# In the first stage's ScalarE step, the normalisation of quad q is put ahead of the message of quad q-1

## The chip, the cores and the metric

The kernel runs on 1 core of a Trainium2 chip. The metric is the device time of one execution in microseconds. The engines are TensorE (PE in the rows; PEld is its weight load), VectorE (DVE), ScalarE (ACT), GpSimd (POOL) and SyncE (SP). Each has its own instruction queue, works through it in order, and meets the others at semaphores only.

## The reference

Two graph layers on 6250 nodes of 256 features and 106,250 edges (`src`, `dst`, a weight each). The first one is a message network:

```python
x1 = concatenate((h[src], h[dst], weight))
msg = silu(x1 @ mW1 + mb1)
msg = layer_norm(msg, ln_g, ln_b)
msg = silu(msg @ mW2 + mb2)
agg = segment_sum(msg, src)
y = silu(concatenate((h, agg)) @ uW1 + ub1) @ uW2 + ub2
x = layernorm(x + h + y)
```

The second takes the mean of `x[src]` over each `dst`, multiplies by `W.T`, adds `b`, applies relu, adds it to `x` and normalises again.

## The kernel before, in words

The edges are sorted by `dst`. A preparation counts them into blocks of 125 nodes, and makes a table `p_tab` of each node's product with one part of mW1, and keeps the products with the other part in `big`. Edges are taken in tiles of 128, and four tiles are a **quad** (`QT` = 4; `QUADS` quads, 220 of them by the count of L973).

The change is in the first stage, the loop over quads. `message_loop(eng, step)` issues, for each engine, the step of every q from -2 to QUADS+2, in unrolled steps at the ends and in loops of four steps between. All buffers named below have two halves, the parity of the quad. For a quad q:

- POOL gathers four times 128 rows of `p_tab` into `gat` (`gather_0`, L572), one step ahead.
- PE multiplies a one-hot by `big` (`expand`, L762), one step ahead; DVE adds it to the gathered rows and writes `act` (`pre`, L1346), at the end of its step before.
- ACT applies silu to `act` in two halves (`silu`, L949).
- DVE takes the statistics (`bn_stats`, L1356), then a chain of small instructions on 128x4 values (`inverse_root`, L360 to L376) ends in `shift` (L1380). Between the links of the chain stand other jobs of DVE's step: `stage` and `one_hot` for quad q+2, `buckets` for q+1, `place` for q-1 (the rows to which the messages go), and `message_sum`.
- ACT applies scale and shift (`norm`, four instructions, L955).
- PE transposes `act` in eight pieces (`norm_columns`, L749) in its step q+1; ACT brings the two halves to `zt` with gain and bias (its own `norm_columns`, L964); PE multiplies by mW2 (`main`, L774 and L775).
- ACT applies the last silu and writes `msg` (`message`, L972 and L973); POOL scatters it to `msg_tab` (`place_messages`, L582).

PE's step q is, in order: `norm_columns(q-1)`, `expand(q+1)`, `rank(q)` (L736, L738), `main(q-1)`. ACT's step q is: silu half 0 of q, half 0 of `norm_columns(q-1)`, silu half 1, half 1 of `norm_columns(q-1)`, `message(q-1)`, `norm(q)`. `message(q-1)` waits until `main(q-1)` has ended (`mm`), and until the scatters of quad q-3 have landed (`add`). `norm(q)` waits for `shift` of q.

From quad `SWITCH` (108) the sorted messages of the first part are also summed beside the steps, in **visits**, from quad 112 on. Three visits stand in every even step, two in every odd one (`SHARE`). A visit is a load by SP (L469), two one-hots on DVE (L1461), four products on PE (`collect`, L802) and an addition on DVE (`message_sum`, L1481). PE has its collects behind `norm_columns`, behind `expand` and, the third, behind `main`. DVE has its three sums behind the statistics, in the chain, and, the third, right ahead of `shift`.

Behind the loop come the rest of the visits, the update network on 50 blocks, the second layer and the output. The change touches none of these.

Of the kernel before, what the change touches and what calls it, by code (L numbers as in the profile page):

```python
# [28 lines left out]
QUADS = -(-(TILES + BLOCKS - 1) // QT)  # L29
# [31 lines left out]
def gnn(nc, x, src, dst, edge_w, mW1, mb1, ln_g, ln_b, mW2, mb2, uW1, ub1, uW2, ub2, W, b, out):  # L61
# [13 lines left out]
    with ExitStack() as ctx:  # L75
# [269 lines left out]
        def live(q, n):  # L345

            return not isinstance(q, int) or 0 <= q < n
# [5 lines left out]
        def later(q, n):  # L353

            return not isinstance(q, int) or q >= n
# [570 lines left out]
        def _(ac):  # L926
# [20 lines left out]
            def silu(q, par, v):  # L947
                ac.wait_ge(s["pre"], 2 * q + v + 1)
                nc.scalar.activation(act[:, par, 2 * v:2 * v + 2, :], act[:, par, 2 * v:2 * v + 2, :], ACT.Silu)\  # L949
                    .then_inc(s["silu"], 1)  # L950

            def norm(q, par):
                ac.wait_ge(s["shift"], q + 1)
                for u in range(QT):
                    last = nc.scalar.activation(act[:, par, u, :], act[:, par, u, :], ACT.Identity,  # L955
                                                bias=shift[:, par, u:u + 1], scale=nwt[:, par, 3, u:u + 1])
                last.then_inc(s["norm"], 1)

            def norm_columns(q, par, h):

                ac.wait_ge(s["ztr"], 2 * q + h + 1)
                if h == 0 and later(q, 2):
                    ac.wait_ge(s["mm"], q - 1)
                nc.scalar.activation(zt[:, par, h, :], ps[:, PZ + h, :], ACT.Identity,  # L964
                                     bias=gb[:, h, 1:2], scale=gb[:, h, 0:1]).then_inc(s["zev"], 1)

            def message(q, par):
                ac.wait_ge(s["mm"], q + 1)
                if later(q, 2):
                    ac.wait_ge(s[f"add{par}"], half_count(q - 2) * (16 * QT))  # L970
                    ac.sem_inc(s_turn_act, 1)
                nc.scalar.activation(msg[:, par, :, D], vkey[:, bass.ds(q * QT, QT)], ACT.Copy).then_inc(s["msg"], 1)  # L972
                nc.scalar.activation(msg[:, par, :, 0:D],  # L973
                                     ps[:, PM:PM + 2, :].rearrange("p b (u d) -> p (b u) d", u=2), ACT.Silu)\
                    .then_inc(s["msg"], 1)

            def step_0(q, par, group):
                for i in range(2):
                    if live(q, QUADS):
                        silu(q, par, i)  # L980
                    if live(q - 1, QUADS):
                        norm_columns(q - 1, 1 - par, i)
                if live(q - 1, QUADS):
                    message(q - 1, 1 - par)
                if live(q, QUADS):
                    norm(q, par)
            ac.wait_ge(s_weights, 16 * 14)
            message_loop(ac, step_0)

            ac.wait_ge(s["qexp"], QUADS)  # L990
# [635 lines left out]
```

## Time and profile before

| | us |
|---|---|
| median of 3 runs | 5003.13 (5003.01 to 5013.02) |
| the profiled execution's own time | 5005.49 |
| its span | 5003.7 |
| PE busy in the span | 3701.3 (74%) |
| DVE busy | 2915.6 (58%) |
| POOL busy | 2583.9 (52%) |
| ACT busy | 1379.0 (28%) |

The mean granted clock of TensorE over the span was 0.858 of full speed. The messages L973, one in each quad, start between 258.3 and 3177.8 us, so the loop over quads holds some 2920 us of the span. In the page's slices PE is busy in seven tenths nearly throughout it, no other engine in more than six tenths. In the chain that ended last PE has 62% of the span and ACT 10%, of which `norm` (L955) has 8%. A busy share is a mean over steps of some 12 to 14 us; which engine is waited for is seen in the order of time in one such step.

### The profile page before, as it was taken

To read this page: it belongs to the slowest core of one execution; us is meant where nothing else is said; L and a number is where in the kernel's file an instruction comes from. 1 tells how busy PE (TensorE), PEld (TensorE's weight loads), DVE (VectorE), ACT (ScalarE), POOL (GpSimd) and SP (SyncE) were. 2 spreads that over 40 slices of the span, in tenths; PEclk is the share of its full clock that TensorE was granted. 3 is DMA by queue.
4 is the path that set the end of the run, shared out by engine and by line. 5 is a ranking of instruction groups with operands and counts; after the bars stand their busy time and mean duration, and the time that the engine had idled before them with its cause. 6 is when DMAs were issued, how large, how long until landed. Compare 5 with 4: busy or idle time off the path is not lost.

```text
span 5003.7 us, 78162 instructions
## 1 busy us (share of the span) xinstructions
PE 3701.3 (74%) x15597; PEld 2734.1 (55%) x15598; DVE 2915.6 (58%) x11562; ACT 1379.0 (28%) x2573; POOL 2583.9 (52%) x2725
## 2 busy tenths in 40 slices
PE   6877777777777777777777777677894777777775
PEld 3455555555555566666666666455583444444444
DVE  5655555555555666666666666466555555545555
ACT  0244444444444444444444444100030000000003
POOL 0066556565565555555555555100004777777753
PEclk9987777777777889999889999899997888888888
DMA  2333222332332444444444444666403333333323
GB/s 54 103 93 93 90 92 91 92 94 90 91 92 92 124 133 138 137 138 136 137 136 139 137 139 135 160 190 185 143 1 114 105 105 105 105 104 105 105 77 104
DMA packets 281644, 563.52 MB, mean 113 GB/s; under 512 B 57407, under 2 KB 128659, under 8 KB 281583
## 3 DMA queue, kind: packets, MB, share of 16 engines
q0 software_dynamic: 124416, 343.51, 22.6%
q1 hardware_dynamic: 150772, 212.91, 15.0%
q10 hardware_dynamic: 6395, 6.40, 0.6%
q8 instruction: 25, 0.41, 0.0%
q14 instruction: 36, 0.29, 0.0%
HBM read 423.51 MB, written 139.08 MB: 112 GB/s over the span
## 4 chain that ended last, share of the span: by engine, by line
PE 62%; DMA 10%; ACT 10%; issue 9%; DVE 4%; DVEq 2%; POOL 1%; SPq 1%; ACTq 1%; POOLq 0%
PE ps L774 16%; PE ps L762 10%; ACT arena L955 8%; PE ps L881 8%; PE ps L802 8%; PE ps L749 8%; DMA arena<-x_tab,esrc 7%; PE ps L884 2%; PE ps L775 2%; PE ps L711 2%; PE ps L832 2%; DMA arena<-msg_tab 1%; PE ps L738 1%; POOL arena L604 1%; DMA arena<-x_tab 1%
## 5 line engine op out<-in xcount | busy, mean ns | idle before, releaser
L582 POOL DMA_INDIRECT msg_tab<-arena,sidx x880 | 865.3, 983 | 892.8 <-ACT arena L973 662.0
L572 POOL DMA_INDIRECT arena<-p_tab,idx x880 | 864.3, 982 | 556.6 <-DVE idx L1328 288.4
L604 POOL DMA_INDIRECT arena<-x_tab,esrc x832 | 789.2, 949 | 299.1 <-issue 142.9
L749 PE MATMUL ps<-ident,arena 128*128 128x128 f32 x1760 | 388.3, 393 | 727.7 <-ACT arena L955 727.7
L881 PE MATMUL ps<-arena 128*125 x1760 | 661.3, 464 | 337.8 <-DMA arena<-x_tab,esrc 296.1
L774 PE MATMUL ps<-w,arena 128*128 128x256 f32 x3520 | 894.7, 387 | 0.9 <-ACT arena L964 0.9
L1356 DVE BATCH_NORM_STATS2 bst<-arena 128x6 f32<-128x256 f32 x880 | 331.2, 418 | 879.2 <-ACT arena L949 879.1
L749 PEld LDWEIGHTS ps<-ident,arena 128*128 128x128 f32 x1760 | 308.5, 204 | 813.2 <-ACT arena L955 613.7
L802 PE MATMUL ps<-arena 128*125 128x256 f32 x2180 | 640.6, 430 | 122.2 <-DVE arena L1461 92.7
L881 PEld LDWEIGHTS ps<-arena 128*125 128x125 f32 x1760 | 378.9, 225 | 603.3 <-issue 516.9
L774 PEld LDWEIGHTS ps<-w,arena 128*128 128x128 f32 x3520 | 608.4, 193 | 125.0 <-ACT arena L964 1.3
L1575 DVE TENSOR_TENSOR arena<-ps,arena 125x257 f32 x880 | 374.7, 426 | 516.3 <-PE ps L881 471.5
L762 PE MATMUL ps<-arena 126*128 x1760 | 586.9, 493 | 8.9 <-DVE arena L1346 5.8
L802 PEld LDWEIGHTS ps<-arena 128*125 128x125 f32 x2180 | 431.7, 215 | 275.1 <-issue 107.6
L762 PEld LDWEIGHTS ps<-arena 126*128 126x128 f32 x1760 | 441.0, 258 | 94.5 <-issue 9.9
L972 ACT ACTIVATE arena<-vkey 128x4 f32 (+1 forms) x220 | 45.9, 209 | 1562.2 <-PE ps L775 1562.2
L955 ACT ACTIVATE arena<-arena,shift,nwt 128x256 f32<-128x256 f32 x880 | 454.2, 589 | 10.0 <-DVE shift L1380 5.7
L1461 DVE TENSOR_SCALAR arena<-nodes,cboff,arena 128x125 f32<-128x125 bf16 x1090 | 337.2, 357 | 118.3 <-DMA arena<-msg_tab 46.5
L884 PE MATMUL ps<-identh 128*128 128x512 bf16 x880 | 396.0, 450 | 0.0
L964 ACT ACTIVATE arena<-ps,gb 128x512 f32<-128x512 f32 x440 | 340.6, 774 | 135.7 <-PE ps L749 135.6
L1027 ACT ACTIVATE arena<-ps 128x250 f32<-128x250 f32 x50 | 18.6, 373 | 1128.7 <-DVE cnt L1591 1128.7
L1481 DVE TENSOR_TENSOR arena<-ps,arena 125x256 f32 x545 | 229.8, 422 | 157.9 <-PE ps L802 154.4
(199 smaller groups left out, 4248.0 us busy)
## 6 DMA issues: line engine op xcount, KB each, us to landing
arena<-msg_tab SPq DMA_DIRECT2D x545, 264.0 KB
arena<-loc_tab SPq DMA_DIRECT2D x220, 125.0 KB
arena<-p_tab,idx POOLq DMA_INDIRECT x880
msg_tab<-arena,sidx POOLq DMA_INDIRECT x880
arena<-x_tab,esrc POOLq DMA_INDIRECT x832, 2.8
arena<-x_tab SPq DMA_DIRECT2D x50, 128.0 KB, 2.0
arena<-in_x_dram SPq DMA_DIRECT2D x50, 112.0 KB
p_tab<-arena SPq DMA_DIRECT2D x50, 112.0 KB
```

What stands on the lines that cost most here:

```text
L572: pool.indirect_dma_start(out=gat[:, par, u, 0:D], out_offset=None, in_=p_tab[:, :], in_offset=bass.IndirectOffsetOnAxis(ap=idx[:, par, u: ...
L582: pool.indirect_dma_start(out=msg_tab[part][:, :], in_=msg[:, par, u, :], in_offset=None, out_offset=bass.IndirectOffsetOnAxis(ap=sidx[:, ...
L604: pool.indirect_dma_start(out=ring[:, tile % RING, 0:D], out_offset=None, in_=x1_tab[:, :], in_offset=bass.IndirectOffsetOnAxis(ap=esrc[:, ...
L749: last = nc.tensor.transpose(ps[:, PZ + h, u * P:(u + 1) * P], act[:, par, u, h * P:(h + 1) * P], ident[:, :])
L762: last = nc.tensor.matmul(ps[:, PP + u // 2, u % 2 * D:(u % 2 + 1) * D], hott[0:NB + 1, par, u, :], big[0:NB + 1, bass.ds(blocks_[u], 1), ...
L774: nc.tensor.matmul(to, zt[:, par, h, u * P:(u + 1) * P], w2[:, h, :], start=h == 0, stop=False)
L802: last = nc.tensor.matmul(ps[0:NB, bank, 0:D], chot[:, j % 2, i, :], crow[:, j % CSLOTS, i, 0:D], start=i == 0, stop=i == 1)
L881: nc.tensor.matmul(ps[0:NB, u, 0:CW], same1[:, par, u, :], ring[:, bass.ds(at[u], 1), :].rearrange("p a c -> p (a c)"), start=True, stop=T ...
L884: nc.tensor.matmul(ps[:, PK, :], identh[:, :], identh[:, :].unsqueeze(1).to_broadcast([P, QT, P]), start=True, stop=True)
L955: last = nc.scalar.activation(act[:, par, u, :], act[:, par, u, :], ACT.Identity, bias=shift[:, par, u:u + 1], scale=nwt[:, par, 3, u:u + 1])
L964: nc.scalar.activation(zt[:, par, h, :], ps[:, PZ + h, :], ACT.Identity, bias=gb[:, h, 1:2], scale=gb[:, h, 0:1]).then_inc(s["zev"], 1)
L1575: nc.vector.tensor_tensor(row, ps[0:NB, u, 0:CW], row, ALU.add).then_inc(s["acc"], 1)
```

## The change

```diff
@@ -980,10 +980,10 @@
                         silu(q, par, i)
                     if live(q - 1, QUADS):
                         norm_columns(q - 1, 1 - par, i)
+                if live(q, QUADS):
+                    norm(q, par)
                 if live(q - 1, QUADS):
                     message(q - 1, 1 - par)
-                if live(q, QUADS):
-                    norm(q, par)
             ac.wait_ge(s_weights, 16 * 14)
             message_loop(ac, step_0)
```

No instruction is added or removed, and no wait. In ACT's queue the wait for `shift` of quad q and the four instructions of `norm(q)` now stand ahead of the waits and the two instructions of `message(q-1)`.

## Rows read from the trace of the kernel before

**Rows 1.** Who waited for whom, 300 to 1600 us: total us, times, longest.

```profile
ACT arena L972 <- PE ps L775: 680.2, 100, 7.3
PE ps L749 <- ACT arena L955: 347.9, 100, 3.5
```

**Rows 2.** Order of time, ACT (start us, us): messages of quads 0, 108, 120, 216.

```profile
258.34 1.01 ACT L973 ACTIVATE arena<-ps 128x1024 f32<-128x1024 f32 x1
...
1657.93 1.01 ACT L973 ACTIVATE arena<-ps 128x1024 f32<-128x1024 f32 x1
...
1828.00 1.01 ACT L973 ACTIVATE arena<-ps 128x1024 f32<-128x1024 f32 x1
...
3138.45 1.01 ACT L973 ACTIVATE arena<-ps 128x1024 f32<-128x1024 f32 x1
```

**Rows 3.** Order of time, all engines, a step at a high granted clock.

```profile
1504.24 0.21 ACT L972 ACTIVATE arena<-vkey 128x4 f32 x1 [7.32 <-PE ps L775]
...
1505.26 2.06 ACT L955 ACTIVATE arena<-arena,shift,nwt 128x256 f32<-128x256 f32 x4
...
1507.22 0.62 ACT L949 ACTIVATE arena<-arena 128x512 f32<-128x512 f32 x1
...
1507.38 1.97 PE L749 MATMUL ps<-ident,arena 128*128 128x128 f32 x8 [3.45 <-ACT arena L955]
...
1508.53 0.78 ACT L964 ACTIVATE arena<-ps,gb 128x512 f32<-128x512 f32 x1 [0.69 <-PE ps L749]
...
1509.20 0.62 ACT L949 ACTIVATE arena<-arena 128x512 f32<-128x512 f32 x1
...
1514.93 0.16 DVE L1380 SCALAR_TENSOR_TENSOR shift<-mom,nwt 128x4 f32<-128x4 f32 x1
...
1515.60 0.27 PE L775 MATMUL ps<-b2r,ones 128*128 128x256 bf16 x1
```

**Rows 4.** Order of time, all engines, a step at a low granted clock.

```profile
1415.27 1.97 PE L749 MATMUL ps<-ident,arena 128*128 128x128 f32 x8 [3.46 <-ACT arena L955]
...
1417.11 0.62 ACT L949 ACTIVATE arena<-arena 128x512 f32<-128x512 f32 x1
...
1422.66 0.16 DVE L1380 SCALAR_TENSOR_TENSOR shift<-mom,nwt 128x4 f32<-128x4 f32 x1
...
1425.13 0.27 PE L775 MATMUL ps<-b2r,ones 128*128 128x256 bf16 x1
```

**Rows 5.** Groups of instructions, 300 to 1600 us: busy us, mean ns, idle before.

```profile
L582 POOL DMA_INDIRECT msg_tab<-arena,sidx x399 | 392.5, 984 | 375.0 <-ACT arena L973 268.7 <-issue 105.8 <-DVE idx L1328 0.6
L572 POOL DMA_INDIRECT arena<-p_tab,idx x400 | 388.1, 970 | 145.5 <-issue 129.9 <-DVE idx L1328 15.6
```

**Rows 6.** Line 572: duration min/median/max in ns, first and last start.

```profile
L572 POOL DMA_INDIRECT arena<-p_tab,idx x880: 942/963/1193, 230.9 to 3136.7; - x176
```

**Rows 7.** Order of time, all engines, a step with two visits.

```profile
2802.67 0.62 ACT L949 ACTIVATE arena<-arena 128x512 f32<-128x512 f32 x1
...
2805.12 1.10 PE L802 MATMUL ps<-arena 128*125 128x256 f32 x4
...
2810.02 0.16 DVE L1380 SCALAR_TENSOR_TENSOR shift<-mom,nwt 128x4 f32<-128x4 f32 x1
...
2810.28 0.27 PE L775 MATMUL ps<-b2r,ones 128*128 128x256 bf16 x1
```

**Rows 8.** Order of time, all engines, the next step, with three visits.

```profile
2813.86 0.62 ACT L949 ACTIVATE arena<-arena 128x512 f32<-128x512 f32 x1
...
2824.29 0.27 PE L775 MATMUL ps<-b2r,ones 128*128 128x256 bf16 x1
...
2825.57 0.42 DVE L1481 TENSOR_TENSOR arena<-ps,arena 125x256 f32 x1 [1.59 <-PE ps L802]
...
2826.10 2.08 ACT L955 ACTIVATE arena<-arena,shift,nwt 128x256 f32<-128x256 f32 x4
...
2828.23 1.97 PE L749 MATMUL ps<-ident,arena 128*128 128x128 f32 x8 [2.80 <-ACT arena L955]
```

## The prediction

> **What bounds the kernel now.** I read the table of waits first, to see which engines stand still in the loop over quads and for whom, then the order of time of single steps, to see which wait ends last. The waits name a pair: ACT stands 6.8 us of each step before `message` until PE's last product of `main` is there, and PE stands 3.5 us of each step before its transposes until ACT's `norm` is there [rows 1]. Neither is busy with anything then, so the two wait in turn.
>
> The step in rows 3 shows why. PE's `main(q-1)` ends; ACT starts `message(q-1)` at 1504.24, is ready for the next instruction 1.02 later (1505.26), does the four instructions of `norm(q)`, and at 1507.38 PE starts the transposes of q. PE had been idle for 3.45 us [rows 3]. The `shift` that `norm(q)` needs is there earlier: the one of the next step ends at 15.09 (1514.93 + 0.16), while `main` ends at 15.87 (1515.60 + 0.27) [rows 3]. In rows 4 it ends at 22.82, and `main` at 25.40. So what holds `norm` is only that it is queued behind a message that waits for `main`. One step is now PE's work from transposes to the end of `main`, 8.49 us in rows 3 and 10.13 in rows 4 (PE's granted clock differs between them), and 3.45 us of hand-over.
>
> How long a step is: 108 steps from the message at 258.34 to that at 1657.93 make 12.96 us each; 96 steps with visits from 1828.00 to 3138.45 make 13.65 us each [rows 2]. The 12 between them are the change-over.
>
> **The change, part by part.** It adds and removes no instruction, and moves no DMA on ACT's queue, since neither function issues one.
>
> *The hand-over goes.* `norm(q)` runs while PE is in `main(q-1)`, and PE's transposes of q can follow `main(q-1)` at once if `norm` has ended. That would be worth 3.45 us less what is late next. Four things can be.
>
> *ACT and DVE as a ring.* `message(q-1)` now stands between `norm(q)` and the silu of q+1, and everything DVE does for q+1 begins with that silu. Its length, if nobody waits for PE: message 1.02 (1504.24 to 1505.26); silu half 0 to silu half 1, 1.29 (1.98 from 1507.22 to 1509.20, less the 0.69 that the L964 between them waited for transposes, which will be ready by then as the message gives them 1.02 more); silu half 1 to the end of shift, 5.89 in rows 3 (1509.20 to 1515.09) and 5.71 in rows 4, I take 5.8; norm to the next instruction, 1.96 (1505.26 to 1507.22) [rows 3, 4]; some 0.04 from shift to norm. Sum 10.1 us. Before, this ring had no message in it and about 3 us of slack.
>
> *PE.* Without waits 8.5 to 10.1 us a step [rows 3, 4]. It has a shorter pause, so I expect it nearer to the first; at the second it would equal the ring.
>
> *POOL.* Each step it issues four scatters (0.984 each) and four gathers (0.970). Its gaps that aren't a wait for ACT are 1.06 us for the scatters ((375.0 - 268.7) / 100 steps) and 1.46 us for the gathers (145.5 / 100) [rows 5], and the first scatter needs one as well, 0.3 by the same rows. 3.93 + 3.88 + 1.06 + 1.46 + 0.3 = 10.6 us. A few long gaps are in that; at eight gaps of 0.31 it is 10.3. It is now hidden behind the 12.96, and isn't after. The scatters of q-1 also become ready later by the length of `norm`. `message(q-1)` waits for the scatters of q-3, and DVE's `pre` for gathers issued a whole step before: both have most of a step of room, so POOL decides by its rate, and not by a single late transfer.
>
> *The message's other customers.* PE's `main(q)` waits for `message(q-1)`, as both use the same banks. The message now ends some 1 us after the transposes of q start, and `main(q)` comes at least 4 us after that start. Covered.
>
> So three limits lie together, 10.1, up to 10.1, and 10.3 to 10.6. For steps without visits I take 10.5 us, in the range 10.2 to 11.2. The saving is 108 x (12.96 - 10.5) = 266 us.
>
> *Steps with two visits.* Silu half 1 to the end of shift is 7.51 (2802.67 to 2810.18), so the ring is 1.02 + 1.29 + 7.51 + 0.04 + 1.96 = 11.8 us. PE: the second collect waits for DVE's sum, 2.45 behind silu half 1 (2802.67 to 2805.12), and `main` ends 5.43 behind its start (2810.55) [rows 7]. Silu half 1 now starts 2.16 after the transposes (1.02 + 1.29 - 0.15), so `main` ends at 2.16 + 2.45 + 5.43 = 10.0. The ring decides: 11.8.
>
> *Steps with three visits.* Here `shift` comes behind the third sum, and this waits for the third collect, which PE has behind `main` [rows 8]. `norm` can't pass `main` here, and the hand-over stays: from the end of `main` at 2824.56 over the collect, the sum, shift and norm to the transposes at 2828.23 is 3.67 us, as before. The message was hidden beside the collect, and now stands in the ring. The step is 10.0 + 3.7 = 13.7 us.
>
> The mean is 12.8, against 13.65: 96 x 0.87 = 84 us. The 12 steps of the change-over (four without visits at about 1.3, eight at 0.87) give 12 and the last three 2. All other stages stay.
>
> Sum: 266 + 84 + 14 = 364 us off the profiled execution's own time, 5005.5 (span 5003.7 and 1.8 around it): 4641. The median of before is 2.4 us below that execution; I call 4641 for the median as well.
>
> *A rule against it.* The longest gather took 1193 ns against a median of 963 [rows 6], with the same code, so something beside it delays it at times. The Trainium skill, SBUF — State Buffer, "Who interferes with whom", says that VectorE in some modes (copy, cast and tensor_scalar, or with two inputs in SBUF) and GpSimd lock each other out of a port pair for a whole instruction. By that rule DVE and POOL, packed into a shorter step, would meet more often, and POOL would come out dearer than its rows of before say. What that would make of the time stands below, out of the rows.
>
> **The rivals.**
>
> *POOL's issue becomes a harder bound than its rows say.* For: its 10.3 to 10.6 is already above the ring. Against: it issues the same eight, and its median of 963 is near its minimum of 942 [rows 6]. At 1.10 and a gap of 0.30 each, eight make 11.2 us: 108 x 1.76 = 190, with the 98 of the rest 288 less, 4717. Chance 0.18.
>
> *The three-visit steps pay for the message.* From silu half 0 to the end of shift such a step took 12.20 us (2813.86 to 2826.06) [rows 8]. If this length is the engines' own and not mostly a wait for PE, the ring is 1.02 + 12.2 + 0.04 + 1.96 = 15.2 us, and the two kinds make 13.5 in the mean. Then the visits give 96 x 0.15 = 14, and the sum is 266 + 14 + 8 = 288, again 4717. For: no wait of DVE but the 1.59 before L1481 is seen. Against: that very wait says that DVE was early, by more than the 1.02 now added. Chance 0.11.
>
> *Slower: the ring gets longer than the old step.* The new step is 3.02 us plus the time from silu half 0 to the end of shift. That time is 7.87 in rows 3. The new order loses from 9.94 on (12.96 - 3.02). If POOL and DVE in each other's way stretch it to 10.3, the steps take 13.3: 108 x 0.36 = 39 us slower, and some 20 more with the visits, 5065. For: the ring has DVE's many short instructions in it. Against: their number doesn't grow, and 2.4 us is a third of all of it. Chance 0.04.
>
> *Nothing happens.* If `norm` is held by something that the waits don't name, say DVE's next quad, the time stays at 5003. Against: shift ended before main in both steps [rows 3, 4]. Chance 0.02.
>
> **How the numbers follow.** The forecast of 4641 has 0.65. Its own range comes from 10.2 to 11.0 without visits and 12.3 to 13.2 with: 4560 to 4735. The range I give is 4565 to 4760, which takes in most of the two rivals at 4717. About 0.2% (10 us) is what a measurement can tell from no change; faster by more than that 0.94, within it 0.02, slower 0.04.
>
> **What would show it.** In the steps without visits: the messages 10.5 us apart; PE idle before L749 for under 2 us, or not at all; ACT's wait before L955 now for DVE's shift; L972 waiting for PE little or nothing; POOL with nearly no wait for L973. If POOL is the bound, DVE or ACT wait for POOL's landings or the gaps before its scatters are all 0.3. With visits: intervals that alternate between 11.8 and 13.7, and the wait of L1481 for L802 still there in every second step. I would be wrong if the steps without visits took over 11.2 us or under 10.1, or if those with three visits became longer than before.

## The result and the profile after

| | before | after |
|---|---|---|
| median, us | 5003.07 (4 runs) | 4602.95 (4601.56 to 4603.83, 4 runs) |
| ratio, with 95% interval | | 0.9196 (0.918 to 0.9212) |
| span of the profiled execution | 5003.7 | 4599.8 |
| mean granted clock of TensorE | 0.858 | 0.917 |

The forecast was 4641. The kernel became 403.9 us shorter by its spans, where 364 were forecast.

The waits of the changed kernel, from 300 to 1350 us (total us, times, longest), beside [rows 1]:

```profile
ACT arena L955 <- DVE shift L1380: 490.0, 103, 5.1
PE ps L749 <- ACT arena L955: 249.5, 102, 3.0
...
DVE arena L1346 <- DMA arena<-p_tab,idx: 36.4, 24, 2.4
...
ACT arena L972 <- PE ps L775: 0.4, 1, 0.4
```

ACT's 6.8 us of waiting for `main` in each step are gone (0.4 in all). It now waits 4.8 us for `shift`. PE still waits for `norm`, 2.4 us instead of 3.5, where I had expected under 2. The hand-over is gone, and what PE waits for is a ring in which it has no part (`norm`, message, silu, DVE's chain).

The messages of quads 0, 108, 120, 216 and 219 in the changed kernel, beside [rows 2]:

```profile
255.96 1.01 ACT L973 ACTIVATE arena<-ps 128x1024 f32<-128x1024 f32 x1
...
1358.98 1.01 ACT L973 ACTIVATE arena<-ps 128x1024 f32<-128x1024 f32 x1
...
1513.93 1.00 ACT L973 ACTIVATE arena<-ps 128x1024 f32<-128x1024 f32 x1
...
2742.52 1.01 ACT L973 ACTIVATE arena<-ps 128x1024 f32<-128x1024 f32 x1
...
2773.03 1.01 ACT L973 ACTIVATE arena<-ps 128x1024 f32<-128x1024 f32 x1
```

| stretch | before, us a step | after | forecast | taken off, us | forecast |
|---|---|---|---|---|---|
| 108 steps without visits | 12.96 | 10.21 | 10.5 | 296.6 | 266 |
| 12 steps of the change-over | 14.17 | 12.91 | | 15.1 | 12 |
| 96 steps with visits | 13.65 | 12.80 | 12.8 | 81.9 | 84 |
| the last three | 13.1 | 10.2 | | 8.9 | 2 |

Those make 402.5; the first message starts 2.4 us earlier and all behind the last takes 0.9 longer, which gives the 403.9.

One step without visits, in the order of time (beside [rows 3, 4]):

```profile
899.55 2.08 ACT L955 ACTIVATE arena<-arena,shift,nwt 128x256 f32<-128x256 f32 x4 [5.09 <-DVE shift L1380]
...
901.53 0.19 ACT L972 ACTIVATE arena<-vkey 128x4 f32 x1
...
901.68 1.09 PE L749 MATMUL ps<-ident,arena 128*128 128x128 f32 x8 [3.01 <-ACT arena L955]
...
902.53 0.62 ACT L949 ACTIVATE arena<-arena 128x512 f32<-128x512 f32 x1
...
903.72 0.62 ACT L949 ACTIVATE arena<-arena 128x512 f32<-128x512 f32 x1
...
908.95 0.27 PE L775 MATMUL ps<-b2r,ones 128*128 128x256 bf16 x1
...
909.54 0.16 DVE L1380 SCALAR_TENSOR_TENSOR shift<-mom,nwt 128x4 f32<-128x4 f32 x1
...
909.74 2.07 ACT L955 ACTIVATE arena<-arena,shift,nwt 128x256 f32<-128x256 f32 x4 [4.74 <-DVE shift L1380]
```

The ring can be read off: message 1.00 (901.53 to 902.53), silu half to silu half 1.19, on to the end of `shift` 5.98 (909.70), 0.04 to `norm`, and `norm` 1.98 (899.55 to 901.53), 10.19 in all. In the mean of quads 5 to 105 it is 2.99 for `norm` and message, 1.18 between the silu halves, 6.02 to the end of `shift` and 0.035 to `norm`. That is 10.22 in all (unrounded), the step itself. In 97 of these 100 steps all but the part on DVE are the same within 0.02 us. So the ring is what holds the changed kernel here. `main` ends at 909.22, before `shift`. From its transposes at 901.68 that is 7.54 us, at a high granted clock.

POOL's groups from 300 to 1350 us (beside [rows 5]):

```profile
L582 POOL DMA_INDIRECT msg_tab<-arena,sidx x409 | 405.9, 992 | 125.5 <-issue 114.2 <-DVE idx L1328 8.5 <-ACT arena L973 2.7
L572 POOL DMA_INDIRECT arena<-p_tab,idx x408 | 394.2, 966 | 124.3 <-issue 114.9 <-ACT arena L973 5.2 <-DVE idx L1328 4.3
```

POOL's wait for the message has fallen from 2.7 us a step to 0.03, and all its gaps are some 0.31. Four scatters, four gathers and eight gaps make 3.97 + 3.86 + 8 x 0.306 = 10.28 us: in these steps POOL has no idle time left. That is a little more than a step takes, and POOL falls behind. Its first scatter of a quad starts 1.9 us behind the start of the quad's message at quad 0, and 9.0 us behind it at quad 108. DVE's waits for gathers in the table above begin at 1083 us only.

A step with three visits, and the start of the next with two (beside [rows 7, 8]):

```profile
1977.15 0.62 ACT L949 ACTIVATE arena<-arena 128x512 f32<-128x512 f32 x1
...
1979.60 1.10 PE L802 MATMUL ps<-arena 128*125 128x256 f32 x4 [0.81 <-DVE arena L1481]
...
1984.76 0.27 PE L775 MATMUL ps<-b2r,ones 128*128 128x256 bf16 x1
...
1986.05 0.43 DVE L1481 TENSOR_TENSOR arena<-ps,arena 125x256 f32 x1 [0.97 <-PE ps L802]
...
1986.57 2.08 ACT L955 ACTIVATE arena<-arena,shift,nwt 128x256 f32<-128x256 f32 x4 [8.13 <-DVE shift L1380]
...
1988.70 1.97 PE L749 MATMUL ps<-ident,arena 128*128 128x128 f32 x8 [2.80 <-ACT arena L955]
...
1998.38 2.07 ACT L955 ACTIVATE arena<-arena,shift,nwt 128x256 f32<-128x256 f32 x4 [6.36 <-DVE shift L1380]
```

From the end of `main` (1985.03) to the transposes (1988.70) it is still 3.67 us. `norm` starts are 11.81 apart over the step with two visits (1986.57 to 1998.38). In the mean of the 96 steps the messages are 11.87 and 13.72 apart in turn. The third sum still waits for the third collect, 0.97 us instead of 1.59.

### The profile page after: what moved, and what is told of

Its sections match the earlier page's. It is cut to its first block, busy times and chain, and to the rows that moved or that the text cites. A ratio compares the mean times of both kernels' runs of the same rounds, so it can differ in the third digit from the quotient of the medians.

```text
span 4599.8 us, 78162 instructions
## 1 busy us (share of the span) xinstructions
PE 3448.3 (75%) x15597; PEld 2513.7 (55%) x15598; DVE 2939.3 (64%) x11562; ACT 1348.7 (29%) x2573; POOL 2577.9 (56%) x2725
## 4 chain that ended last, share of the span: by engine, by line
PE 31%; DVE 18%; ACT 17%; issue 15%; DMA 11%; DVEq 3%; POOL 2%; SPq 1%; ACTq 1%; POOLq 0%
PE ps L881 8%; DMA arena<-x_tab,esrc 8%; ACT arena L955 6%; PE ps L802 6%; PE ps L774 4%; ACT arena L949 3%; ACT arena L973 3%; ACT arena L964 3%; PE ps L884 3%; PE ps L711 2%; PE ps L832 2%; DVE arena L1461 2%; POOL arena L604 2%; DVE nwt L376 1%; DVE nwt L370 1%
## 5 line engine op out<-in xcount | busy, mean ns | idle before, releaser
L572 POOL DMA_INDIRECT arena<-p_tab,idx x880 | 853.6, 970 | 497.5 <-issue 256.9
L955 ACT ACTIVATE arena<-arena,shift,nwt 128x256 f32<-128x256 f32 x880 | 456.5, 590 | 1325.5 <-DVE shift L1380 1325.5
L802 PE MATMUL ps<-arena 128*125 128x256 f32 x2180 | 624.1, 421 | 169.6 <-DVE arena L1461 95.1
L881 PEld LDWEIGHTS ps<-arena 128*125 128x125 f32 x1760 | 378.1, 225 | 603.6 <-issue 516.8
L749 PE MATMUL ps<-ident,arena 128*128 128x128 f32 x1760 | 283.1, 312 | 506.8 <-ACT arena L955 506.8
L802 PEld LDWEIGHTS ps<-arena 128*125 128x125 f32 x2180 | 410.8, 205 | 329.3 <-DVE arena L1461 160.6
L749 PEld LDWEIGHTS ps<-ident,arena 128*128 128x128 f32 x1760 | 223.0, 159 | 591.8 <-ACT arena L955 468.5
L762 PE MATMUL ps<-arena 126*128 x1760 | 455.7, 405 | 16.5 <-DVE arena L1346 13.2
L762 PEld LDWEIGHTS ps<-arena 126*128 126x128 f32 x1760 | 355.8, 208 | 75.9 <-issue 21.2
L964 ACT ACTIVATE arena<-ps,gb 128x512 f32<-128x512 f32 x440 | 337.1, 766 | 0.7 <-PE ps L749 0.7
L1346 DVE TENSOR_TENSOR arena<-ps,arena 128x512 f32<-128x512 f32 x440 | 283.0, 685 | 78.4 <-DMA arena<-p_tab,idx 44.8
L597 POOL MEMSET arena<- 125x257 f32 x50 | 15.7, 314 | 557.6 <-PE ps L824 557.5
```

The source lines that it names most:

```text
L572: pool.indirect_dma_start(out=gat[:, par, u, 0:D], out_offset=None, in_=p_tab[:, :], in_offset=bass.IndirectOffsetOnAxis(ap=idx[:, par, u: ...
L749: last = nc.tensor.transpose(ps[:, PZ + h, u * P:(u + 1) * P], act[:, par, u, h * P:(h + 1) * P], ident[:, :])
L762: last = nc.tensor.matmul(ps[:, PP + u // 2, u % 2 * D:(u % 2 + 1) * D], hott[0:NB + 1, par, u, :], big[0:NB + 1, bass.ds(blocks_[u], 1), ...
L802: last = nc.tensor.matmul(ps[0:NB, bank, 0:D], chot[:, j % 2, i, :], crow[:, j % CSLOTS, i, 0:D], start=i == 0, stop=i == 1)
L881: nc.tensor.matmul(ps[0:NB, u, 0:CW], same1[:, par, u, :], ring[:, bass.ds(at[u], 1), :].rearrange("p a c -> p (a c)"), start=True, stop=T ...
```

## Experiments

**e1: the message a whole step later.**

```diff
+                if live(q - 2, QUADS):
+                    message(q - 2, par)
                 if live(q, QUADS):
                     norm(q, par)
-                if live(q - 1, QUADS):
-                    message(q - 1, 1 - par)
```

> The changed kernel, with ACT's message a whole step later: in its step q it does silu, the transposed halves, then message(q-2), then norm(q). The message then lies in the time in which ACT waits for shift, and is out of the ring silu - DVE chain - norm - silu. Theory A (steps without visits are held by two limits side by side, the ring at 10.1 us and POOL's issue at 10.2 to 10.3): they stay at 10.2 to 10.3. Steps with two visits, which the ring alone holds, go from 11.8 to 10.8, those with three from 13.6 to about 13.1 (silu, sum and second collect 1.0 earlier, as far as PE is there). Together 96 x 0.75 = 72 us less than the changed kernel's 4603: about 4530. Theory B (the ring alone holds the steps without visits): these go to 9.2, and the time to about 4425. Theory C (POOL alone holds them): as A here; the next two runs tell A and C apart.

Measured 4543.59 (before, on the same chip, 5005.33; ratio 0.9076, 0.9055 to 0.9096). The messages of quads 0, 108, 120 and 216:

```profile
261.84 1.02 ACT L973 ACTIVATE arena<-ps 128x1024 f32<-128x1024 f32 x1
...
1379.05 1.02 ACT L973 ACTIVATE arena<-ps 128x1024 f32<-128x1024 f32 x1
...
1526.57 1.02 ACT L973 ACTIVATE arena<-ps 128x1024 f32<-128x1024 f32 x1
...
2686.72 1.02 ACT L973 ACTIVATE arena<-ps 128x1024 f32<-128x1024 f32 x1
```

With visits the steps take 12.08 instead of 12.80. The ring without its message gives 0.7 of the message's 1.0: a step with two visits comes to 11.2 and not to the 10.8 that I expected, one with three to 13.0. Silu half 1 comes 1.60 us behind half 0, and in the changed kernel 1.18. The transposes now follow `norm` with no message between, and ACT's L964 waits for them (29.1 us in 94 times from 1530 to 2680 us). Without visits they take 10.34, so a shorter ring gives nothing there (theory B falls). What DVE waits for now tells the bound (waits, 300 to 1200 us):

```profile
DVE arena L1346 <- DMA arena<-p_tab,idx: 152.0, 65, 2.6
```

That is the landing of POOL's gathers; in the changed kernel it was 36.4 us in a longer stretch. Behind it ACT's silu stands and waits for `pre` (L949 for L1346: 97.3 us in 87 times), which it doesn't do in the table of the changed kernel. So here it is POOL that sets the step.

**e2: three gathers instead of four.** Before the loop POOL sets the rows of the fourth tile to zero.

```diff
-                for u in range(QT):
+                for u in range(QT - 1):
                     pool.indirect_dma_start(
                         out=gat[:, par, u, 0:D], out_offset=None, in_=p_tab[:, :],
...
-                dve.wait_ge(s[f"gat{par}"], half_count(q) * (16 * QT))
+                dve.wait_ge(s[f"gat{par}"], half_count(q) * (16 * (QT - 1)))
```

> The changed kernel, with three of POOL's four gathers in each step; the rows of the fourth tile are zero, so a quarter of the gathered rows is left out of the computation. POOL's issue of a step falls by one gather and its gap, 1.26 us, to 9.0 us; the ring stays. Theory A (both limits side by side): steps without visits go from 10.2 only to the ring's 10.1, steps with visits stay; 4603 less about 12, 4591. Theory B (ring alone): no change, 4600. Theory C (POOL alone): steps without visits 9.0 to 9.2, about 4490.

Measured 4586.50 (ratio 0.9164, 0.9145 to 0.9183). Messages of quads 0 and 108 (L973 is L975 in this file):

```profile
256.00 1.01 ACT L975 ACTIVATE arena<-ps 128x1024 f32<-128x1024 f32 x1
...
1345.21 1.01 ACT L975 ACTIVATE arena<-ps 128x1024 f32<-128x1024 f32 x1
```

10.09 us a step: 1.26 us less work on POOL gave 0.12. Theory C falls. The 0.12 lies in DVE's part of the ring, from silu half 1 to the end of `shift`: 5.89 in the mean here, 6.02 in the changed kernel. Why is said below.

**e3: both.** The edits of e1 and e2 together.

> Both edits of the two runs before: message a step later, and three gathers (a quarter of the gathered rows left out). Theory A: only now do the steps without visits fall, to about 9.2 us (ring 9.1, POOL 9.0, PE 8.5 or less at a high clock): 110 us less than the kernel with the later message alone, about 4420. Theory B: no more than the later message alone (about 4425 there and here). Theory C: no more than three gathers alone gave in these steps. If PE's own work were a limit near 10 us, all of these would stay at 10.

Measured 4459.05 (ratio 0.8911, 0.8893 to 0.8929). Messages of quads 0 and 108:

```profile
260.58 1.02 ACT L975 ACTIVATE arena<-ps 128x1024 f32<-128x1024 f32 x1
...
1292.54 1.02 ACT L975 ACTIVATE arena<-ps 128x1024 f32<-128x1024 f32 x1
```

9.56 us a step. Each edit alone left these steps at 10.1 to 10.3; both together took them 0.5 to 0.8 below either. So there are two limits side by side, which is theory A. That it stopped at 9.56 and not 9.2 is a miss of mine by 39 us in the total. The trace tells where the 0.4 is. In the order of time (L957, L951, L966 and L751 are L955, L949, L964 and L749 of the other files):

```profile
703.50 2.08 ACT L957 ACTIVATE arena<-arena,shift,nwt 128x256 f32<-128x256 f32 x4 [3.65 <-DVE shift L1382]
...
705.62 1.09 PE L751 MATMUL ps<-ident,arena 128*128 128x128 f32 x8 [1.50 <-ACT arena L957]
...
706.32 0.78 ACT L966 ACTIVATE arena<-ps,gb 128x512 f32<-128x512 f32 x1 [0.23 <-PE ps L751]
707.00 0.62 ACT L951 ACTIVATE arena<-arena 128x512 f32<-128x512 f32 x1
```

The ring closes in each step here too: in the mean of quads 5 to 105, 0.04 from `shift` to `norm`, 1.98 to the silu, 1.56 to its second half and 5.96 to `shift`, 9.54 in all. I had taken 1.29 and 5.8 for the last two. The 1.29 was worked out with the message ahead of the silu, which gave the transposes their time; without it L966 waits for them. PE also stands 0.66 us before `main` for the late message (62.7 us in 95 times, L776 for L975). That isn't in the ring: PE is early for its transposes, and waits another 1.50 for `norm`.

**e4: the third sum behind shift.** Of DVE's step, in the changed kernel:

```diff
-                    if i in (2, 7, 15) and len(group) > (2, 7, 15).index(i):
-                        at = (2, 7, 15).index(i)
+                    if i in (2, 7) and len(group) > (2, 7).index(i):
+                        at = (2, 7).index(i)
...
                     norm(q, par, beside)
+                    if len(group) == 3:
+                        message_sum(*group[2], to[2], PC)
```

> The changed kernel, with DVE's third message_sum of a step (which waits for PE's collect behind main) moved from ahead of shift to behind it. My theory: in steps with three visits norm can't pass main because shift waits for that sum; without it they become like those with two, 11.8 to 12.1 instead of 13.6 us. 48 such steps x 1.6 = 77 us less than 4603: about 4526. Rival: the three-visit steps are long because of DVE's and PE's own work (another sum, two more one-hots, another collect); then they stay over 13 us, and the time stays within 15 us of 4603.

Measured 4496.99 (ratio 0.8988, 0.8969 to 0.9006). Messages of quads 120 and 216:

```profile
1500.44 1.00 ACT L973 ACTIVATE arena<-ps 128x1024 f32<-128x1024 f32 x1
...
2639.47 1.01 ACT L973 ACTIVATE arena<-ps 128x1024 f32<-128x1024 f32 x1
```

11.86 us in the mean: the steps with three visits have become as short as those with two. 90 us of the 106 lie in these 96 steps, 14 in the change-over (141.0 us instead of 155.0), which I hadn't counted. No engine has less to do in this kernel; the three visits were not dear, but their last sum stood ahead of `shift`.

**e10: the old order in the steps with three visits only.**

```diff
+                if len(group) == 3:
+                    message(q - 1, 1 - par)
                 if live(q, QUADS):
                     norm(q, par)
-                if live(q - 1, QUADS):
+                if len(group) != 3 and live(q - 1, QUADS):
                     message(q - 1, 1 - par)
```

This kernel (as e7) and three others first ran on a chip of which more is said below; e9 to e12 are their second runs, on another one.

> The kernel of e7 again (old order in steps with three visits only), for the same reason. Steps with two visits fall from 11.8 to about 11.2, those with three stay at 13.6: about 4572 where the changed kernel takes 4603. Rival: 4603.

Measured 4564.24 (before there 4997.53; ratio 0.9128, 0.9107 to 0.9149). Messages of quads 144, 145 and 146:

```profile
1808.17 1.01 ACT L973 ACTIVATE arena<-ps 128x1024 f32<-128x1024 f32 x1
1818.58 1.01 ACT L973 ACTIVATE arena<-ps 128x1024 f32<-128x1024 f32 x1
...
1833.16 1.01 ACT L973 ACTIVATE arena<-ps 128x1024 f32<-128x1024 f32 x1
```

This pair takes 24.99 us, and 24.81 is the mean of all 48 pairs, instead of 25.6; 24.8 was expected. Where `norm` waits behind `main` anyway, the new order costs a message's time in the next step's ring.

**e12: before, with the third sum behind shift.** The edit of e4 on the kernel before.

> The kernel of e8 again: the kernel before with the third message_sum behind shift. My theory: norm stays behind main by the queue order, so only some 11 us and up to 14 of the change-over go: 4980 to 4995 where before takes 5003. Rival: the third sum costs 1.6 us under either order; about 4925.

Measured 5003.00 (before there 5007.76; ratio 0.9992, 0.9981 to 1.0002). Order of time, messages of quads 120 and 216:

```profile
1817.47 1.01 ACT L973 ACTIVATE arena<-ps 128x1024 f32<-128x1024 f32 x1
...
3127.85 1.01 ACT L973 ACTIVATE arena<-ps 128x1024 f32<-128x1024 f32 x1
```

13.65 us a step, as before; the change-over gave 6. The rival (1.6 us under either order) falls. The 11 us that I expected of the shorter hand-over did not come either. The same edit is worth 106 us behind the new order and no more than some 10 ahead of it.

**e9 and e11: the causes together.** e9 has the edits of e1 and e4. e11 has them too, but in steps without visits the message stands where the changed kernel has it:

```diff
+                later_message = len(group) > 0 or isinstance(q, int) and q >= QUADS
+                if later_message and live(q - 2, QUADS) and not (isinstance(q, int) and q == SWITCH + 4):
+                    message(q - 2, par)
                 if live(q, QUADS):
                     norm(q, par)
-                if live(q - 1, QUADS):
+                if not later_message and live(q - 1, QUADS):
                     message(q - 1, 1 - par)
```

> The kernel of e5 again (message a whole step later, third message_sum behind shift): its first run fell on a chip on which the kernel before itself takes 5379 us and engines stand still at other places. On a chip on which before takes about 5003: as told for e5, about 4445, steps with visits 11.2 us in the mean. Rival: another limit near 11.8 holds them; 4490. If before is again far from 5003, the ratio to it will be near 1, and tells only of that chip.

> The kernel of e6 again: the message a step later only in the steps with visits, third sum behind shift. e9 took 4433. With the 10.21 us of the changed kernel in the steps without visits instead of 10.34: 14 us less, about 4420. Rival: the place of the message has no part in the 0.13; 4433.

Measured: e9 4432.98 (before 4997.53; ratio 0.8872, 0.885 to 0.8893), e11 4421.05 (before 5007.76; ratio 0.8833, 0.8818 to 0.8848). Both take 11.11 us a step with visits, nearly every one within 0.07 of it. Without visits e9 takes 10.33 and e11 10.22. POOL's gathers in these steps (groups, 300 to 1300 us, e9 and then e11):

```profile
L572 POOL DMA_INDIRECT arena<-p_tab,idx x385 | 384.9, 1000 | 117.3 <-issue 117.3
```

```profile
L572 POOL DMA_INDIRECT arena<-p_tab,idx x389 | 375.3, 965 | 118.5 <-issue 109.1 <-ACT arena L973 5.8 <-DVE idx L1331 3.7
```

A gather is 35 ns dearer in e9 and a scatter 10 ns cheaper (982 against 992), so POOL's eight take 0.10 us more: about the 0.11 between the two. The 35 ns are those of a few gathers: in e9 68 of the 385 took 1.10 to 1.17 us, and each of the 68 began 0.11 to 0.17 us behind the start of DVE's L365; in e11 5 of 389 were so long. e11 is the fastest version here, 182 us below the changed kernel by the medians.

**e5 to e8: the same four kernels on a chip that behaved otherwise.**

> The changed kernel with both edits: message a whole step later, and the third message_sum behind shift. Alone they gave 4544 and 4497. My theory (ring, and shift held by the third sum, are separate causes): steps with visits come to about 11.2 us in the mean (ring 10.8; with three visits up to 11.5, since DVE's pre now stands behind the third sum), from 12.08; with the 14 us of the change-over that the second edit gave, 4544 - 85 - 14 = about 4445. Steps without visits stay at 10.34 (POOL). Rival: another limit near 11.8 holds the steps with visits (PE with three collects, or DVE); then it stays at 4490.

> As the run before, but the message is a step later only in the steps with visits; in those without it stands behind norm(q), as in the changed kernel. Those steps then take the changed kernel's 10.21 us instead of 10.34: 108 x 0.13 = 14 us less than the run before, about 4430. Rival: the 0.13 comes from something else than the message's place (it was seen in one kernel only); then the time is that of the run before.

> The changed kernel, but in steps with three visits ACT's message stands ahead of norm, as before the change. There shift comes over 1 us behind the end of main, so the message costs norm nothing, and the silu of the next quad comes 1.0 us earlier. My theory: the next step (two visits) is held by the ring and falls from 11.8 to about 11.2 (silu half 1 then waits for transposes at a low clock, up to 0.7); the three-visit ones stay at 13.6. 48 x 0.65 = 31 us less than 4603: about 4572. Rival: the message is no part of what sets these steps; 4603.

> The kernel before (message ahead of norm), with the third message_sum behind shift. My theory: norm is then held by the message behind main in every step; a three-visit step's hand-over falls from 3.67 only to 3.45 us. 48 x 0.22 = 11 us, and up to 14 of the change-over: 4980 to 4995. Rival: the third sum costs its 1.6 us under either order; then about 4925.

On this chip the kernel before took 5379.16 (12 runs). e5 took 5457.48 (ratio 1.0146, 1.0129 to 1.0163), e6 5451.94 (1.0125, 1.0108 to 1.0142), e7 5365.48 (0.9971, 0.996 to 0.9982), e8 5361.66 (0.9964, 0.995 to 0.9978). The waits of e8, which elsewhere is as fast as before, hold this:

```profile
ACT arena L972 <- remote: 383.4, 47, 9.8
...
DVE arena L1577 <- remote: 235.9, 82, 6.6
```

The traces of the same four kernels on the other chip (e9 to e12) and that of the kernel before have no wait of this kind. L1577 is a line of the second layer, so it isn't the first stage alone. In e5 ACT's L964 waited 483.1 us in 123 times in this way. The releaser is none that the profile names, and the waits fall at other places in each kernel. I can't say what they are, nor whether the changed kernel itself would be faster than before on such a chip: it was not run there. One and the same kernel has the ratio 0.9971 here (e7) and 0.9128 on the other chip (e10). No step of the argument rests on these four runs.

## Why the prediction was right

*The hand-over goes because norm was held by the queue order alone.* Shown: ACT's wait for `main` fell from 6.8 us a step to nothing. The rival "nothing happens" is out.

*The ring with the message in it is the next limit.* Its sum of 10.1 was measured at 10.19 in the step above, at 10.22 in the mean, and at 10.09 where POOL had less to do (e2). In steps with two visits 11.8 was forecast, and 11.81 measured in the step above, 11.87 in the mean. e1 took the message out of it and got 0.72 in the mean of the steps with visits.

*POOL is a second limit beside it.* Shown by e1, e2 and e3 together. But I let POOL set the step, and that is not what the changed kernel does: there the ring closes in every step, and POOL falls behind by some 7 us over the 108. The 10.5 is the mis-sized term of the sum: I had 10.3 to 10.6 for POOL, which measured 10.28, and the step was 10.21. The two limits lie so near each other that the forecast of a step is 3% off and no more, though it names the wrong one: that is luck. The 1.46 us of gaps for four gathers held waits that belong to the slower step (before the first gather of a step, 59 of 0.53 and 17 of 0.92). With all eight at 0.306 the sum is 10.28. 108 x 0.29 = 31 us of the 40 by which the forecast was too long come from this; 7 more from the last three steps.

*PE needed less than I gave it.* I had 8.5 to 10.1 without waits, and it is 7.54 in the step above. So it stands 2.4 us before its transposes, and my sign of under 2 us did not come. Nothing in the sum hung on it, since I had set the step by POOL.

*Three-visit steps keep their hand-over.* Shown: 3.67 us before and after; e4 takes out the sum that holds it. The rival that these steps pay for the message in full (15.2 us) is out: most took 13.6, some 14.2. DVE's wait of 1.59 before L1481 had room for it, and shrank to 0.97. In part it was right all the same: e10 shows that the message does cost there, 0.4 us a step in the mean of the pair.

*POOL as a harder bound (11.2).* Out: the gather's mean was 970 ns before [rows 5] and 966 after, its maximum 1193 [rows 6] and 1192. By the rule of the Trainium skill (SBUF — State Buffer, "Who interferes with whom") a denser step could have made it dearer. The changed kernel's gathers don't show that; the 68 long ones of e9 would fit it, as L365 is a `tensor_scalar`. It is DVE that paid in the changed kernel, and this I had not counted in the sum. L360, a `tensor_scalar` too, in the kernel before (300 to 1600 us) and in the changed one (300 to 1350 us; duration min/median/max in ns):

```profile
L360 DVE TENSOR_SCALAR nwt<-mom x100: 169/169/171, 300.5 to 1588.4; 128x4 int32<-128x4 int32 x100
```

```profile
L360 DVE TENSOR_SCALAR nwt<-mom x103: 169/171/409, 301.1 to 1343.2; 128x4 int32<-128x4 int32 x103
```

*Slower.* This rival needed 2.4 us more on DVE's chain. It was stretched by 0.12: silu half 1 to the end of `shift` is 6.02 in the mean, against 5.90 before and 5.89 in e2.

## What to carry to other kernels

In an engine's queue, an instruction whose input is ready and which stands behind one that waits for the slowest engine is worth moving ahead; what it gives is set by the next ring, so add up that ring with the moved instruction in it, and each other engine's issue time with all its gaps at their smallest. When two limits lie within 2% of each other, relieving one shows next to nothing (here 0 and 0.12 us of a step, and 0.65 for both), and only both together tell. An engine without idle time need not be the limit yet: here POOL lagged more and more while the ring set the pace. A wait in the middle of an in-order step (here the third sum ahead of `shift`) may cost nothing under one order and 1.9 us under another, so look again at such places once an order is changed.

## What the runs showed of the hardware

TensorE's granted clock was 0.79 in the steps without visits before and 0.97 after, without any edit on TensorE (a stretch of each kernel, before and after: its length, the busy time and count of PE, its weight load, DVE, ACT and POOL, then granted clock, DMA share and GB/s):

```profile
300.00:1600.00 1300.00, 952.14 (x4100) 758.99 (x4099) 714.46 (x3397) 556.35 (x1000) 779.87 (x799) 0.79 0.30 92
```

```profile
300.00:1350.00 1050.00, 782.08 (x4210) 621.14 (x4208) 746.28 (x3494) 559.35 (x1026) 800.11 (x817) 0.97 0.38 116
```

Before, PE stood idle for 3.45 us ahead of each transposition, after for 2.4 in the mean. The eight transposes took 1.97 us at the lower of its two levels (1.2 GHz) and 1.09 at the higher (2.4 GHz). In the steps without visits before, 84 of 103 had their transposes at the lower level, after 11 of 103. It bought no time in the changed kernel: the steps that begin with such slow transposes took 10.19 us in the mean, the others 10.22. Before, where PE is in the limit, the clock made steps of 11.95 and of 13.6 us out of the same work, and after, nearly all lie between 9.9 and 10.6.

DVE and POOL stretched single instructions of each other. In the changed kernel 39 of the 103 L360 took over 300 ns and not 170:

```profile
895.36 1.00 POOL L582 DMA_INDIRECT msg_tab<-arena,sidx  x1 [0.30 <-issue]
895.92 0.41 DVE L360 TENSOR_SCALAR nwt<-mom 128x4 int32<-128x4 int32 x1
```

All 39 began 0.56 to 0.67 us behind the start of an issue of POOL's, and ended 0.94 to 0.97 us behind it, when that issue was nearly over. Of the other 64 only one began in this stretch (214 ns). In the kernel before and in e2 no L360 (L361 there) took over 172 ns. That such meetings make all of the 0.12 us on DVE's chain was not tried.

One chip took 5379 us for a kernel that takes 5003 on the others, with waits of up to 11.9 us (L972 in e7) for which the profile names no instruction.
